# The first attention of a two-layer gated network: exponentials one step on, projections a tile ahead, a second normalisation on Pool

## The chip, the core and the metric
The kernel runs on one core of a Trainium2 chip. The metric is the device time of one execution in microseconds (us), lower is better. The engines of the core work side by side, each through its own list of instructions in order, and wait for one another through counters (semaphores): TensorE (PE) does matrix products and transposes, VectorE (DVE) and ScalarE (ACT) do work per element, GpSimd (Pool) does slower work per element, and SyncE (SP) issues transfers.

## What is computed
The whole program is a network of two layers, each with a cross-attention and a feed-forward part, on 32 x 64 tokens of width 256. The change touches the first cross-attention alone:

```python
x = x + tanh(g_xattn[0]) * xattn0(layernorm(x), ctx, ctx, W_q, W_k, W_v, W_o)

def xattn0(XQ, XK, XV, Wq, Wk, Wv, Wo):      # projections mix the 64 rows of a batch entry
    q, k, v = heads(Wq @ XQ), heads(Wk @ XK), heads(Wv @ XV)     # 8 heads of 32 columns
    p = softmax(q @ k.T / sqrt(32))
    return Wo @ (XQ - p @ v)
```

So the normalised rows of x are needed twice: once early, for the queries, and once late, where the attention is subtracted from them.

## The kernel before
The 2048 tokens are 16 tiles of 128 rows (two batch entries each). `attention0` (from L303) runs the tiles as a software pipeline. Each engine has a function `step(s)`, which issues what belongs to tile s, and, for the tiles before, t = s-1 and u = s-2; on VectorE n = s+1 is the next tile. `run_steps` (L75) calls it for the first steps, then in a hardware loop over pairs of steps, then for the last ones. Nothing but these functions sets the order: an engine does its instructions as they are written, and waits at each `after(...)` until the counter named there has come far enough.

One tile passes through these operations, whose names are used below:
- **xn** (DVE, L590 through L175): normalised rows for the queries. **Q/K** (PE, L530): projections of queries and keys, 8 matmul instructions. **V** (PE, L536): projection of the values.
- **q_t, k_m** (ACT, L474 and L478): queries and keys from PSUM to SBUF. **v_m** (one half on DVE, L603, one on ACT, L491): the values.
- **scores** (PE, L551), **smax** and **shifted** (DVE, L609 and L612), **prob** (ACT, L500): exponentials. **den, rden** (DVE, L596 and L598): sums and their reciprocals.
- **transposes of prob** (PE, L543), **p_t** (ACT, L483), **out** (PE, L563), **head** (DVE, L638).
- **xn_late** (ACT, L485): the second normalisation, **mix** (Pool, L454): the difference, **proj** (PE, L571), **x_all** and **stats** (DVE, L643 and L645): the residual and the statistics of the next norm.

Beside this, ACT and Pool split the context into two parts for the second attention (k_hi, L496; k_lo, L440), Pool splits the weights of the feed-forward part (w_hi and w_lo, L445 and L447), and SP loads the context and stores the parts. At step 2 the norm of the tiles from 4 on is computed (L617 on DVE, with a square root on ACT at L505).

In a step before the change PE does Q/K(s), V(s), transposes(t), scores(s), out(t), proj(u). ACT does q_t and k_m(s), p_t(t), xn_late(t), v_m(s), k_hi(s), prob(s). DVE does den and rden(t), v_m(s), xn(n), smax and shifted(s), head(t), x_all and stats(u).

Of the kernel before, what the change touches and what calls it, by code (L numbers as in the profile page):

```python
# [10 lines left out]
ALU = mybir.AluOpType  # L11
# [63 lines left out]
def run_steps(eng, body, count, lag, unroll, head=0):  # L75

    head = max(head, -(-lag // unroll))
    tail = count // unroll  # L80
    for n in range(head * unroll):
        body(Step(n // unroll, n % unroll, unroll))
    with eng.Fori(head, tail) as r:
        for slot in range(unroll):
            body(Step(r, slot, unroll))
    for n in range(tail * unroll, count + lag):
        body(Step(n // unroll, n % unroll, unroll))
# [215 lines left out]
def attention0(nc, sem, keep, d):  # L303
# [5 lines left out]
    with ExitStack() as ctx:  # L309
# [103 lines left out]
        def _(pool):  # L413
# [20 lines left out]
            def step(s):  # L434
                if s.inside(TILES):
# [12 lines left out]
                t = s.plus(-1)  # L448
                if t.inside(TILES):

                    after(pool, late_ready, t)
# [8 lines left out]
        def _(act):  # L460
# [8 lines left out]
            def step(s):  # L469
# [10 lines left out]
                if t.inside(TILES):  # L480
                    after(act, pt_done, t)
                    after(act, o_done, t.plus(-2))
                    act.activation(p_t[:, t.slot], pt_ps[:], ACT.Copy).then_inc(pt_ready, 1)  # L483
                    after(act, mix_ready, t.plus(-2))
                    act.activation(xn_late[:, t.slot], at(x_all, t.n), ACT.Identity, bias=column(norm.shift, t.n),  # L485
                                   scale=column(norm.rstd, t.n)).then_inc(late_ready, 1)
                if s.inside(TILES):
                    after(act, v_done, s)
# [4 lines left out]
                if s.inside(TILES):  # L493
                    after_dma(act, ctx_loaded, s)
                    after_dma(act, kop_written, s.plus(-2), 3)
                    act.activation(k_hi[:, s.slot], ctx_t[:, s.slot], ACT.Copy).then_inc(khi_ready, 1)  # L496
                    after(act, shift_ready, s)
                    after(act, pt_done, s.plus(-2))
                    after(act, den_ready, s.plus(-2))
                    act.activation(prob[:, s.slot], shifted[:, s.slot], ACT.Exp, scale=SCALE0).then_inc(prob_ready, 1)  # L500
                    if s.known and s.n == 0:
                        act.wait_ge(gate_loaded, 48)
                        act.activation(gates[:], gate_in[:, 0:4], ACT.Tanh).then_inc(gate_steps, 1)
                    if s.known and s.n == 2:
                        norm.scalar(act, slice(GT, XT))  # L505
# [5 lines left out]
        def _(pe):  # L511
# [6 lines left out]

            def step(s):
                t, u = s.plus(-1), s.plus(-2)  # L520
                if s.inside(TILES):

                    after(pe, xn_ready, s)
                    after_dma(pe, ctx_loaded, s)
                    after(pe, q_ready, s.plus(-2))
                    after(pe, k_ready, s.plus(-2))
                    for m, src in ((0, xn), (1, ctx_t)):
                        for c in range(DC):
                            o = (2 * m + c) * P
                            mm = pe.matmul(qk_ps[s.slot][:, o:o + P], lhsT=src[:, s.slot, c * P:(c + 1) * P], rhs=w_t[:, m],  # L530
                                           start=True, stop=True)
                    mm.then_inc(qk_done, 1)
                    after(pe, v_ready, s.plus(-1))
                    after(pe, v_odd_ready, s.plus(-1))
                    for b in range(2):
# [1628 lines left out]
```

## Time and profile before
| | |
|---|---|
| median of 3 runs | 675.91 us (674.12 to 676.22) |
| profiled execution | 673.21 us, of which 671.5 us are the span |
| first attention | from the start to about 106 us |
| loop over tile pairs, steps 4 to 15 | about 40 to 101 us |
| busy of each step of 5.12 us (two steps, 41.0 to 51.3 us, halved) | PE 4.40, DVE 4.15, ACT 4.35, Pool 2.89 us |

The trace gives for each group of instructions its start, its length, its engine and its line; in square brackets stands how long the engine was idle before it and what ended that. "issue" is idle time for which the profile shows no releaser. A group of several instructions starts with the first and ends with the last. The matmul clock that the chip granted was full speed from 40 to 90 us, and 0.89 and 0.77 of it in the two stretches of 5 us before that.

### The profile page before, as it was taken

How to read it: one execution, taken by the hardware profiler on the slowest of the kernel's cores; microseconds unless marked ns; L12 is line 12 of the kernel's file. 1: busy time of each engine (PE TensorE's matmuls, PEld its weight loads, DVE VectorE, ACT ScalarE, POOL GpSimd, SP SyncE). 2: the span in 40 equal slices, each digit the busy share in tenths (PEclk: the TensorE clock that was granted, in tenths of full speed). 3: DMA queues.
4: the chain of work that ended last, by engine and by line, in shares of the span. 5: the costliest groups of instructions: out<-in, count | busy, mean ns of one | idle time of the engine just before them, and what ended most of it. 6: DMA issues, size and time to landing. Idle time of an engine off the chain costs nothing. (4 is left out here: it accounts for less than half of the span.)

```text
span 671.5 us, 16680 instructions
## 1 busy us (share of the span) xinstructions
PE 603.9 (90%) x4997; PEld 460.1 (69%) x4997; DVE 489.4 (73%) x999; ACT 404.1 (60%) x829; POOL 313.0 (47%) x430
## 2 busy tenths in 40 slices
PE   3688877999999966999999999999789699999995
PEld 2577765788888865655555555555478599999884
DVE  2877886788978796598899999996556634444756
ACT  3888884344434441488898888998645145555431
POOL 2455555023222557934675765753237334024254
PEclk9989997999999987699999999999969889999998
DMA  5434438400000014344444444440002435446344
GB/s 163 114 99 130 130 105 290 155 1 1 0 0 1 23 50 137 106 132 130 129 145 127 138 139 123 143 139 29 2 1 75 130 102 187 145 150 189 109 141 127
DMA packets 72601, 71.20 MB, mean 106 GB/s; under 512 B 12364, under 2 KB 68812, under 8 KB 72556
## 3 DMA queue, kind: packets, MB, share of 16 engines
q1 hardware_dynamic: 67324, 56.33, 28.2%
q0 software_dynamic: 5232, 14.29, 6.9%
q8 instruction: 25, 0.41, 0.3%
q14 instruction: 20, 0.16, 0.1%
HBM read 38.48 MB, written 31.36 MB: 104 GB/s over the span
## 5 line engine op out<-in xcount | busy, mean ns | idle before, releaser
L1420 DVE TENSOR_REDUCE a_smax<-a_s 128x2 f32<-128x512 f32 x256 | 164.7, 681 | 19.9 <-PE a_s L1348 15.1
L1242 ACT ACTIVATE a_prob<-a_st 128x512 f32<-128x512 f32 x256 | 141.8, 597 | 23.8 <-PE a_st L1343 22.7
L1348 PE MATMUL a_s<-kop,qop 64*128 64x256 f32 x512 | 106.3, 324 | 5.6 <-DVE a_smax L1420 3.4
L1343 PEld LDWEIGHTS a_st<-qop,kop 64*128 64x128 f32 x512 | 70.8, 187 | 56.8 <-issue 24.9
L1343 PE MATMUL a_st<-qop,kop 64*128 64x256 f32 x512 | 104.0, 315 | 0.6 <-DVE a_smax L1420 0.5
L1303 PE MATMUL a_pv<-a_prob,a_vt 128*32 128x256 f32 x1024 | 81.6, 391 | 3.2 <-ACT a_pv_sb L1227 1.7
L819 POOL TENSOR_TENSOR f_hs_lo<-f_kept,f_hs_hi 128x512 fp32r<-128x512 f32 x32 | 41.3, 1320 | 85.5 <-ACT f_hs_hi L769 85.5
L1348 PEld LDWEIGHTS a_s<-kop,qop 64*128 64x128 f32 x512 | 73.0, 193 | 7.9 <-DVE a_smax L1420 4.8
L1871 POOL DMA_INDIRECT sorted_rows<-m_xn,m_slot x32 | 33.5, 1047 | 46.1 <-PE m_gu L128 26.6
L126 PE MATMUL f_bank<-f_xt_hi,w_hi 128*128 128x512 f32 x128 | 51.2, 400 | 1.1 <-DVE w_raw L865 0.6
L127 PE MATMUL f_bank<-f_xt_lo,w_hi 128*128 128x512 f32 x128 | 50.5, 395 | 0.0
L128 PE MATMUL f_bank<-f_xt_hi,w_lo 128*128 128x512 f32 x128 | 50.3, 393 | 0.0
L787 ACT ACTIVATE f_mag<-w_raw 128x512 f32<-128x512 f32 x32 | 20.2, 633 | 44.5 <-DVE w_raw L865 44.5
L1181 POOL TENSOR_TENSOR we_lo<-we_raw,we_hi 128x176 f32 (+3 forms) x24 | 16.5, 688 | 61.5 <-DMA qop<-qop_rows 57.6
L126 PE MATMUL f_bank<-wd_hi,f_hs_hi 128*128 128x256 f32 x128 | 37.4, 292 | 6.3 <-POOL f_hs_lo L819 6.2
L1887 POOL DMA_INDIRECT m_xn<-expert_rows,m_slot x16 | 15.9, 993 | 54.5 <-DMA expert_rows<-turned 39.5
L865 DVE TENSOR_TENSOR w_raw<-f_sg,f_bank 128x512 f32<-128x512 f32 x32 | 21.9, 684 | 21.3 <-ACT f_sg L783 15.6
L127 PE MATMUL f_bank<-wd_lo,f_hs_hi 128*128 128x256 f32 x128 | 36.9, 288 | 0.0
L128 PE MATMUL f_bank<-wd_hi,f_hs_lo 128*128 128x256 f32 x128 | 36.9, 288 | 0.0
L1303 PEld LDWEIGHTS a_pv<-a_prob,a_vt 128*32 128x32 f32 x1024 | 20.6, 107 | 22.1 <-ACT a_pv_sb L1227 3.7
L783 ACT ACTIVATE f_sg<-f_bank 128x512 f32<-128x512 f32 x32 | 18.7, 585 | 27.0 <-PE f_bank L128 27.0
L440 POOL TENSOR_TENSOR k_lo<-ctx_t,k_hi 128x256 fp32r<-128x256 f32 x16 | 11.7, 729 | 47.2 <-ACT k_hi L496 34.9
(263 smaller groups left out, 1663.4 us busy)
## 6 DMA issues: line engine op xcount, KB each, us to landing
qop<-qop_rows SPq DMA_DIRECT2D x64, 100.0 KB
kop<-kop_rows SPq DMA_DIRECT2D x64, 96.0 KB
sorted_rows<-x_all SPq DMA_DIRECT2D x2, 2944.0 KB, 15.4
qop<-sorted_rows SPq DMA_DIRECT2D x46, 128.0 KB, 2.3
expert_rows<-turned SPq DMA_DIRECT2D x46, 128.0 KB
kop_rows<-k_hi SPq DMA_DIRECT2D x32, 128.0 KB, 2.3
qop_rows<-q_hi POOLq DMA_DIRECT2D x30, 128.0 KB, 2.7
x_all<-in_x SPq DMA_DIRECT2D x4, 512.0 KB, 5.8
```

The costliest lines, as they stand in the source:

```text
L126: pe.matmul(out, lhsT=lh, rhs=rh, start=first, stop=False, **kw)
L127: pe.matmul(out, lhsT=lh, rhs=rl, start=False, stop=False, **kw)
L128: return pe.matmul(out, lhsT=ll, rhs=rh, start=False, stop=last, **kw)
L787: act.activation(mag[:, j], hid[:, c, j], ACT.Abs).then_inc(mag_ready, 1)
L819: pool.tensor_tensor(hs[1][:, j], kept[:, j], raw(hs[0][:, j]), ALU.subtract).then_inc(hs_ready, 1)
L865: dve.tensor_tensor(hid[:, c, j], sg[:, j % 2], u_ps[j % 2][:], ALU.mult).then_inc(hid_ready, 1)
L1242: act.activation(prob[:, u % 8], st_ps[BANK[u]][:], ACT.Exp, scale=SCALE1).then_inc(prob_ready, 1)
L1303: mm = pe.matmul(pv_ps[v4 * 32:(v4 + 1) * 32, 0:D], lhsT=vt[:, w_.slot, c, u], rhs=prob[:, u % 8, c * D:(c + 1) * D], start=(c == 0), stop ...
L1343: st = pe.matmul(st_ps[BANK[u]][:, c * D:(c + 1) * D], lhsT=kop[t.slot][rows, u // 2, c * P:(c + 1) * P], rhs=qop[t.slot][rows, u // 2], s ...
L1348: sm = pe.matmul(s_ps[BANK[u]][:, c * D:(c + 1) * D], lhsT=qop[v.slot][rows, w // 2, c * P:(c + 1) * P], rhs=kop[v.slot][rows, w // 2], st ...
L1420: dve.tensor_reduce(smax[:, v.slot, opposite(u)], s_ps[BANK[u]][:].rearrange("p (q n) -> p q n", q=2), AX_X, ALU.max).then_inc(smax_ready, 1)
L1871: pool.indirect_dma_start(out=d["sorted"][b], out_offset=bass.IndirectOffsetOnAxis(ap=slot[:, k, t:t + 1], axis=0), in_=xn[:, t], in_offse ...
```

## The change
It has four parts.
- PE issues Q/K and V of tile n = s+1 within step s: Q/K(n) behind scores(s), V(n) behind transposes(t). Those of tile 0 stand ahead of the steps, and `run_steps` ends the loop one pair earlier on PE (`ahead=2`).
- ACT issues prob for t = s-1 instead of s, right behind q_t and k_m(s). k_hi and v_m follow, and p_t(t) is last.
- xn_late leaves ACT. Pool makes it from two operations (a product with 1/std and a sum with the shift), at the start of its step.
- DVE issues den and rden(t) behind shifted(s) instead of at the start of the step.

```diff
--- before.py
+++ after.py
@@ -72,12 +72,12 @@
         return not self.known or 0 <= self.n < count
 
 
-def run_steps(eng, body, count, lag, unroll, head=0):
+def run_steps(eng, body, count, lag, unroll, head=0, ahead=0):
 
 
 
     head = max(head, -(-lag // unroll))
-    tail = count // unroll
+    tail = (count - ahead) // unroll
     for n in range(head * unroll):
         body(Step(n // unroll, n % unroll, unroll))
     with eng.Fori(head, tail) as r:
@@ -432,6 +432,14 @@
             pool.memset(norm.eps[:], EPS).then_inc(ident_steps, 1)
 
             def step(s):
+                t = s.plus(-1)
+                if t.inside(TILES):
+                    after(pool, xn_ready, t)
+                    after(pool, mix_ready, t.plus(-2))
+                    scale, shift = (column(c, t.n).to_broadcast([P, D]) for c in (norm.rstd, norm.shift))
+                    pool.tensor_tensor(xn_late[:, t.slot], at(x_all, t.n), scale, ALU.mult).then_inc(late_ready, 1)
+                    after(pool, late_ready, t, 2, 1)
+                    pool.tensor_tensor(xn_late[:, t.slot], xn_late[:, t.slot], shift, ALU.add).then_inc(late_ready, 1)
                 if s.inside(TILES):
                     after_dma(pool, w0_loaded, s)
 
@@ -445,10 +453,9 @@
                     pool.tensor_copy(w0[0][:, m, :, :, n], src).then_inc(w0_hi, 1)
                     after(pool, w0_hi, s)
                     pool.tensor_tensor(w0[1][:, m, :, :, n], src, raw(w0[0][:, m, :, :, n]), ALU.subtract).then_inc(w0_lo, 1)
-                t = s.plus(-1)
                 if t.inside(TILES):
 
-                    after(pool, late_ready, t)
+                    after(pool, late_ready, t, 2)
                     after(pool, head_ready, t)
                     after(pool, proj_done, t.plus(-2))
                     pool.tensor_tensor(mix[:, t.slot], xn_late[:, t.slot], head[:, t.slot], ALU.subtract).then_inc(mix_ready, 1)
@@ -478,31 +485,28 @@
                         op = act.activation(k_m[r, s.slot, :, :, h], src, ACT.Copy)
                     op.then_inc(k_ready, 1)
                 if t.inside(TILES):
-                    after(act, pt_done, t)
-                    after(act, o_done, t.plus(-2))
-                    act.activation(p_t[:, t.slot], pt_ps[:], ACT.Copy).then_inc(pt_ready, 1)
-                    after(act, mix_ready, t.plus(-2))
-                    act.activation(xn_late[:, t.slot], at(x_all, t.n), ACT.Identity, bias=column(norm.shift, t.n),
-                                   scale=column(norm.rstd, t.n)).then_inc(late_ready, 1)
+                    after(act, shift_ready, t)
+                    after(act, pt_done, t.plus(-2))
+                    after(act, den_ready, t.plus(-2))
+                    act.activation(prob[:, t.slot], shifted[:, t.slot], ACT.Exp, scale=SCALE0).then_inc(prob_ready, 1)
+                    if t.known and t.n == 0:
+                        act.wait_ge(gate_loaded, 48)
+                        act.activation(gates[:], gate_in[:, 0:4], ACT.Tanh).then_inc(gate_steps, 1)
                 if s.inside(TILES):
+                    after_dma(act, ctx_loaded, s)
+                    after_dma(act, kop_written, s.plus(-2), 3)
+                    act.activation(k_hi[:, s.slot], ctx_t[:, s.slot], ACT.Copy).then_inc(khi_ready, 1)
                     after(act, v_done, s)
                     after(act, o_done, s.plus(-2))
                     for out, src in v_copies(s, 1):
                         op = act.activation(out, src, ACT.Copy)
                     op.then_inc(v_odd_ready, 1)
-                if s.inside(TILES):
-                    after_dma(act, ctx_loaded, s)
-                    after_dma(act, kop_written, s.plus(-2), 3)
-                    act.activation(k_hi[:, s.slot], ctx_t[:, s.slot], ACT.Copy).then_inc(khi_ready, 1)
-                    after(act, shift_ready, s)
-                    after(act, pt_done, s.plus(-2))
-                    after(act, den_ready, s.plus(-2))
-                    act.activation(prob[:, s.slot], shifted[:, s.slot], ACT.Exp, scale=SCALE0).then_inc(prob_ready, 1)
-                    if s.known and s.n == 0:
-                        act.wait_ge(gate_loaded, 48)
-                        act.activation(gates[:], gate_in[:, 0:4], ACT.Tanh).then_inc(gate_steps, 1)
-                    if s.known and s.n == 2:
-                        norm.scalar(act, slice(GT, XT))
+                if t.inside(TILES):
+                    after(act, pt_done, t)
+                    after(act, o_done, t.plus(-2))
+                    act.activation(p_t[:, t.slot], pt_ps[:], ACT.Copy).then_inc(pt_ready, 1)
+                if s.known and s.n == 2:
+                    norm.scalar(act, slice(GT, XT))
 
             run_steps(act, step, TILES, 2, 2, 2)
             norm.scalar(act, EARLY)
@@ -516,32 +520,31 @@
             pe.transpose(banks[1][:, 0:P], w_raw[:, 4], ident[:]).then_inc(wt_done, 1)
             pe.wait_ge(wt_ready, 1)
 
+            def queries_and_keys(n):
+                if not n.inside(TILES):
+                    return
+                after(pe, xn_ready, n)
+                after_dma(pe, ctx_loaded, n)
+                after(pe, q_ready, n.plus(-2))
+                after(pe, k_ready, n.plus(-2))
+                for m, src in ((0, xn), (1, ctx_t)):
+                    for c in range(DC):
+                        o = (2 * m + c) * P
+                        mm = pe.matmul(qk_ps[n.slot][:, o:o + P], lhsT=src[:, n.slot, c * P:(c + 1) * P], rhs=w_t[:, m],
+                                       start=True, stop=True)
+                mm.then_inc(qk_done, 1)
+
+            def values(n):
+                if not n.inside(TILES):
+                    return
+                after(pe, v_ready, n.plus(-1))
+                after(pe, v_odd_ready, n.plus(-1))
+                for b in range(2):
+                    mm = pe.matmul(v_ps[:, b * D:(b + 1) * D], lhsT=w_t[:, 3 + b], rhs=ctx_t[:, n.slot], start=True, stop=True)
+                mm.then_inc(v_done, 1)
+
             def step(s):
-                t, u = s.plus(-1), s.plus(-2)
-                if s.inside(TILES):
-
-                    after(pe, xn_ready, s)
-                    after_dma(pe, ctx_loaded, s)
-                    after(pe, q_ready, s.plus(-2))
-                    after(pe, k_ready, s.plus(-2))
-                    for m, src in ((0, xn), (1, ctx_t)):
-                        for c in range(DC):
-                            o = (2 * m + c) * P
-                            mm = pe.matmul(qk_ps[s.slot][:, o:o + P], lhsT=src[:, s.slot, c * P:(c + 1) * P], rhs=w_t[:, m],
-                                           start=True, stop=True)
-                    mm.then_inc(qk_done, 1)
-                    after(pe, v_ready, s.plus(-1))
-                    after(pe, v_odd_ready, s.plus(-1))
-                    for b in range(2):
-                        mm = pe.matmul(v_ps[:, b * D:(b + 1) * D], lhsT=w_t[:, 3 + b], rhs=ctx_t[:, s.slot], start=True, stop=True)
-                    mm.then_inc(v_done, 1)
-                if t.inside(TILES):
-
-                    after(pe, prob_ready, t)
-                    after(pe, pt_ready, t.plus(-1))
-                    for hp in range(4):
-                        mm = pe.transpose(pt_ps[:, hp * P:(hp + 1) * P], prob[:, t.slot, hp * P:(hp + 1) * P], ident[:])
-                    mm.then_inc(pt_done, 1)
+                t, u, n = s.plus(-1), s.plus(-2), s.plus(1)
                 if s.inside(TILES):
                     after(pe, q_ready, s)
                     after(pe, k_ready, s)
@@ -553,6 +556,15 @@
                                            rhs=k_m[:, s.slot, c, b].rearrange("p h e -> p (h e)"),
                                            start=True, stop=True, tile_position=(0, b * SEQ))
                     mm.then_inc(score_done, 1)
+                queries_and_keys(n)
+                if t.inside(TILES):
+
+                    after(pe, prob_ready, t)
+                    after(pe, pt_ready, t.plus(-1))
+                    for hp in range(4):
+                        mm = pe.transpose(pt_ps[:, hp * P:(hp + 1) * P], prob[:, t.slot, hp * P:(hp + 1) * P], ident[:])
+                    mm.then_inc(pt_done, 1)
+                values(n)
                 if t.inside(TILES):
                     after(pe, pt_ready, t)
                     after(pe, v_ready, t)
@@ -570,7 +582,9 @@
                     after(pe, x_ready, u.plus(-1))
                     pe.matmul(proj_ps[:, 0:D], lhsT=w_t[:, 2], rhs=mix[:, u.slot], start=True, stop=True).then_inc(proj_done, 1)
 
-            run_steps(pe, step, TILES, 2, 2)
+            queries_and_keys(Step(0, 0, 2))
+            values(Step(0, 0, 2))
+            run_steps(pe, step, TILES, 2, 2, ahead=2)
 
         @block.vector
         def _(dve):
@@ -591,11 +605,6 @@
 
             def step(s):
                 t, u, n = s.plus(-1), s.plus(-2), s.plus(1)
-                if t.inside(TILES):
-                    after(dve, prob_ready, t)
-                    dve.tensor_reduce(den[:, t.slot], prob[:, t.slot].rearrange("p (h e) -> p h e", h=H0), AX_X, ALU.add).then_inc(den_ready, 1)
-                    after(dve, den_ready, t)
-                    dve.reciprocal(rden[:, t.slot], den[:, t.slot]).then_inc(rden_ready, 1)
                 if s.inside(TILES):
                     after(dve, v_done, s)
                     after(dve, o_done, s.plus(-2))
@@ -612,6 +621,11 @@
                     dve.tensor_tensor(shifted[:, s.slot].rearrange("p (h e) -> p h e", h=H0),
                                       s_ps[s.slot][:].rearrange("p (h e) -> p h e", h=H0),
                                       smax[:, s.slot].unsqueeze(2).to_broadcast([P, H0, SEQ]), ALU.subtract).then_inc(shift_ready, 1)
+                if t.inside(TILES):
+                    after(dve, prob_ready, t)
+                    dve.tensor_reduce(den[:, t.slot], prob[:, t.slot].rearrange("p (h e) -> p h e", h=H0), AX_X, ALU.add).then_inc(den_ready, 1)
+                    after(dve, den_ready, t)
+                    dve.reciprocal(rden[:, t.slot], den[:, t.slot]).then_inc(rden_ready, 1)
                 if s.known and s.n == 2:
                     dve.wait_ge(stats0, TILES)
                     norm.vector(dve, slice(GT, XT), lambda: finished(t, u))
```

What stands on PE in one step of the loop, before. The rows are instructions in order: the line, the operation, the tile written and the ones read, and the shape.
```order
L530 MATMUL a_bank<-w_t,xn 128x128 x2
L530 MATMUL a_bank<-w_t,ctx_t 128x128 x2
L536 MATMUL a_bank<-ctx_t,w_t 128x256 x2
L543 MATMUL a_bank<-ident,prob 128x128 x4
L551 MATMUL a_bank<-k_m,q_t 64x256 x4
L563 MATMUL a_bank<-v_m,p_t 64x64 x8
L571 MATMUL a_bank<-mix,w_t 128x256
```
And after the change (L554 scores, L533 Q/K, L565 transposes, L543 V, L575 out, L583 proj; the ISA rows are the registers and waits of the loop):
```order
L554 MATMUL a_bank<-k_m,q_t 64x256 x4
L94 ISA
L101 ISA
L533 MATMUL a_bank<-w_t,xn 128x128 x2
L533 MATMUL a_bank<-w_t,ctx_t 128x128 x2
L565 MATMUL a_bank<-ident,prob 128x128 x4
L543 MATMUL a_bank<-ctx_t,w_t 128x256 x2
L575 MATMUL a_bank<-v_m,p_t 64x64 x8
L583 MATMUL a_bank<-mix,w_t 128x256
```
Scores come first in the step; Q/K stands behind scores and V behind the transposes, both for the next tile.

What stands on DVE from x_all of one step on into the next, before:
```order
L643 SCALAR_TENSOR_TENSOR x_all<-a_bank,gates,x_all 128x256
L645 ISA
L645 BN_STATS stats<-x_all 128x6
L596 TENSOR_REDUCE den<-prob 128x8
L598 RECIPROCAL rden<-den 128x8
L94 REGISTER_ALU
L603 COPY v_m<-a_bank 64x4x32 x2
L175 ISA x2
L175 TENSOR_SCALAR xn<-x_all,ln_rstd,ln_shift 128x256
L609 TENSOR_REDUCE smax<-a_bank 128x8
```
And after the change (L657 x_all, L659 stats, L612 v_m, L175 xn, L618 smax, L621 shifted, L626 and L628 the sums and reciprocals):
```order
L657 SCALAR_TENSOR_TENSOR x_all<-a_bank,gates,x_all 128x256
L659 ISA
L659 BN_STATS stats<-x_all 128x6
L94 REGISTER_ALU
L612 COPY v_m<-a_bank 64x4x32 x2
L175 ISA x2
L175 TENSOR_SCALAR xn<-x_all,ln_rstd,ln_shift 128x256
L618 TENSOR_REDUCE smax<-a_bank 128x8
L621 TENSOR_TENSOR shifted<-a_bank,smax 128x512
L626 TENSOR_REDUCE den<-prob 128x8
L628 RECIPROCAL rden<-den 128x8
```
The sums and reciprocals have moved from between stats and v_m to behind shifted. xn stands where it stood, behind v_m and ahead of smax, and it is still for tile s+1, which PE now takes in step s.

## Rows read from the trace of the kernel before
**Rows 1.** timeline at 66 us, first path: start us, length us, engine, line
```profile
65.64 1.08 PE L551 MATMUL a_bank<-k_m,q_t 128*64 128x256 f32 x8 [0.76 <-issue]
...
66.76 0.69 DVE L609 TENSOR_REDUCE smax<-a_bank 128x8 f32<-128x512 f32 x1 [0.83 <-PE a_bank L551]
...
67.48 0.69 DVE L612 TENSOR_TENSOR shifted<-a_bank,smax 128x512 f32<-128x512 f32 x1
...
68.21 0.63 ACT L500 ACTIVATE prob<-shifted 128x512 f32<-128x512 f32 x1 [0.66 <-DVE shifted L612]
...
68.86 0.38 ACT L474 ACTIVATE q_t<-a_bank 128x256 f32<-128x256 f32 x1
...
69.14 1.52 ACT L478 ACTIVATE k_m<-a_bank 32x256 f32<-32x256 f32 x4
...
70.69 0.60 ACT L483 ACTIVATE p_t<-a_bank 128x512 f32<-128x512 f32 x1
```

**Rows 2.** timeline, the scores of step 4 (loop entry)
```profile
40.02 1.08 PE L551 MATMUL a_bank<-k_m,q_t 128*64 128x256 f32 x8 [0.73 <-issue]
```

**Rows 3.** timeline, same step, rest of the matmul engine
```profile
66.52 0.66 PE L563 MATMUL a_bank<-v_m,p_t 128*64 128x64 f32 x16
...
67.12 0.70 PE L571 MATMUL a_bank<-mix,w_t 128*128 128x256 f32 x2
...
67.65 0.61 PE L530 MATMUL a_bank<-w_t,xn 128*128 128x128 f32 x4
...
68.10 0.61 PE L530 MATMUL a_bank<-w_t,ctx_t 128*128 128x128 f32 x4
...
68.54 1.03 PE L536 MATMUL a_bank<-ctx_t,w_t 128*128 128x256 f32 x4
...
69.41 0.60 PE L543 MATMUL a_bank<-ident,prob 128*128 128x128 f32 x4
```

**Rows 4.** timeline, same step, rest of the vector engine
```profile
68.09 0.41 DVE L638 TENSOR_TENSOR head<-a_bank,rden 128x256 f32<-128x256 f32 x1
...
68.42 0.47 DVE L643 SCALAR_TENSOR_TENSOR x_all<-a_bank,gates,x_all 128x256 f32 x1
...
69.04 0.43 DVE L645 BATCH_NORM_STATS2 stats<-x_all  x1
...
69.45 0.69 DVE L596 TENSOR_REDUCE den<-prob 128x8 f32<-128x512 f32 x1
...
70.37 0.48 DVE L603 COPY v_m<-a_bank 64x128 f32<-64x128 f32 x2
...
70.78 0.40 DVE L175 TENSOR_SCALAR xn<-x_all,ln_rstd,ln_shift 128x256 f32 x1
```

**Rows 5.** timeline, same step, Pool
```profile
67.63 0.73 POOL L440 TENSOR_TENSOR k_lo<-ctx_t,k_hi 128x256 fp32r<-128x256 f32 x1 [1.99 <-ACT k_hi L496]
...
69.14 0.86 POOL L447 TENSOR_TENSOR w_lo<-w_raw,w_hi  x1 [0.17 <-POOL w_hi L445]
...
69.96 0.73 POOL L454 TENSOR_TENSOR mix<-xn_late,head 128x256 f32<-128x256 f32 x1
```

**Rows 6.** timeline, the same form of Pool operation at 264 us
```profile
264.49 0.61 POOL L203 TENSOR_TENSOR q_lo<-x_all,ln_rstd 128x256 f32<-128x256 f32 x1
```

**Rows 7.** timeline, 478 us, two normalisations with Pool idle
```profile
478.32 0.74 DVE L175 TENSOR_SCALAR a_vt<-x_all,ln_rstd,ln_shift 128x256 f32<-128x256 f32 x2
```

**Rows 8.** timeline, 479 us, the next two, with Pool at work
```profile
478.97 1.73 DVE L175 TENSOR_SCALAR a_vt<-x_all,ln_rstd,ln_shift 128x256 f32<-128x256 f32 x2
479.01 0.73 POOL L1199 TENSOR_TENSOR a_att<-a_back 128x256 f32<-128x256 f32 x1 [5.56 <-ACT a_back L1254]
...
479.82 0.72 POOL L1201 TENSOR_TENSOR x_all<-x_all,a_att 128x256 f32<-128x256 f32 x1
```

**Rows 9.** timeline, step 3 before the loop
```profile
31.09 0.31 ACT L171 ACTIVATE ln_std<-ln_var,eps 128x13 f32<-128x13 f32 x1
...
33.32 1.44 PE L551 MATMUL a_bank<-k_m,q_t 128*64 128x256 f32 x8 [2.43 <-issue]
```

## Prediction
> **What bounds the kernel now.** I read the windows first. From 40 to 90 us no engine is full: in a step of 5.12 us all four compute engines have idle time, so a chain through several engines sets the pace. Then the timeline of one step, in which the brackets name the waits. [rows 1] are that chain: prob (start 68.21) to q_t 0.65, q_t to k_m 0.28, k_m 1.52, k_m's end (70.66) to the next scores 0.10, scores to smax 1.12, smax to shifted 0.72, shifted to prob 0.73. The sum is 5.12 us. From the scores of step 4 at 40.02 [rows 2] to those at 65.64 [rows 1] are five steps of 5.12 us, so the chain closes. It is closed because ACT does prob(s) ahead of q_t and k_m(s+1). The reader should see in [rows 1] that ACT waits 0.66 us for shifted and PE 0.76 us ahead of the scores.
>
> **What the change removes.** prob moves to the next step, behind k_m, so shifted has a whole step to be ready and that chain is open. xn_late leaves ACT, which is not the limit then. These edits give nothing by themselves: what counts is which chain is longest next.
>
> **What is late next: ACT and PE.** p_t(t) is last in ACT's step and waits for transposes(t), which now stand behind scores(s) and Q/K(n); the next q_t stands behind p_t. Lengths from [rows 1, 3]: scores 0.88 (65.64 to 66.52), Q/K 0.89 (67.65 to 68.54), transposes 0.60 and 0.04 to ACT (as from the end of the scores to smax), p_t 0.62 with its hand-over, q_t 0.28, k_m 1.52, to the scores 0.10. Sum 4.93 us, 0.19 less than today. V, k_hi and v_m lie beside it.
>
> **What is late next: xn.** DVE issues xn(n) where it did, behind v_m(s), and that is behind x_all and stats of the step before. Today PE takes xn a step later. Now Q/K(n) wants it in step s, 0.88 us after scores(s) start. x_all(u) waits for proj(u), the last thing in PE's step. So a chain closes: Q/K(n), transposes, V, out, proj, x_all, stats, v_m, xn, next Q/K. Its terms, by [rows 3, 4]:
> Q/K 0.89; transposes 0.45 (not seen with a successor; four matmuls of that shape take 0.45 from 67.65 to 68.10, and at most the 0.60 they last); V 0.87 (68.54 to 69.41); out 0.60 (66.52 to 67.12); proj 0.70 and 0.04 to DVE; x_all to stats 0.62 (68.42 to 69.04); stats to its successor 0.41 (69.04 to 69.45); v_m to xn 0.41 (70.37 to 70.78); xn 0.40; to PE 0.07 (between the 0.04 and the 0.10 above).
> Sum 5.46 us, 0.34 more than today. Queued behind the waiting Q/K on PE are transposes, V, out and proj, and behind these p_t, head and x_all; so the wait costs its full length. den and rden, 0.92 us from 69.45 to 70.37 in [rows 4], have left this stretch; without that move it would be 6.4. They now stand in the time in which DVE waits for out.
>
> **Pool.** Its four operations take 3.06 us, from 67.63 to 70.69 in [rows 5]. xn_late adds two. The same form lasts 0.61 [rows 6], mix of this size 0.73 [rows 5], and the second waits 0.17 for the first, as w_lo does for w_hi [rows 5]. That makes 4.5 to 4.7 us, under 5.46, and mix is wanted only one step later. So Pool's time is hidden, but not its place beside xn. [rows 7] show two operations of xn's kind with Pool idle: 0.74 us. [rows 8] show the next two with Pool at work: 1.73 us. 
> Where does xn fall? Count from the start of head, 0.70 after out starts (0.66 and 0.04). x_all follows at 0.64 (0.60 + 0.70 + 0.04 - 0.70), xn at 0.64 + 0.62 + 0.41 + 0.41 = 2.08. Pool: head 0.41, 0.04 to 0.17 to Pool (the two signal times above), mix 0.73, first half of xn_late 0.61 to 0.73, 0.17: the second half starts at 1.96 to 2.21. xn is held if that is under 2.12, which is about the middle. When held, xn ends 0.15 behind that half, at 2.72 to 3.00 instead of 2.48: 0.24 to 0.52 us more, around 0.35. The two halves of the unrolled loop have different register work, so one parity may be held and the other not. I take half of the steps at 0.3, on average 0.15: a step of 5.61 us. Bounds: 5.46 free, 5.98 held each time at the longest.
>
> **Sum.** From scores(4) to scores(15) are 11 steps: 11 x (5.61 - 5.12) = 5.4 us. Before them: the square root of the norm at step 2 stands ahead of q_t(3) on ACT, and scores(3) follow it [rows 9]. Its vector part now stands behind den and rden, 0.92 us. I take 0.9; bounds 0 (if the slow stretch of the clock around 33 us, scores of 1.44 us in [rows 9], hides it) and 1.8 (if the later out(0) costs as much again). After them: x_all and stats(13), 0.62 and 0.41, now stand ahead of den(15); I take 0.5, bounds 0 and 1.0. What follows the first attention starts when all engines have left it, so a shift there is passed on whole. Total +6.8 us: 673.2 of the profiled execution becomes 680.0. That execution was 2.7 us under the median of the runs, to which the sum is added: 675.9 + 6.8 = **682.7 us**, 1.0% slower. The forecast's own range, with xn held in few or in most steps, is 680 to 685.
>
> **Rivals.**
> - Pool holds xn in every step. For it: [rows 8], and the interval above lies more below 2.12 than above if mix's 0.73 is the right length. Against: the 0.61 of [rows 6], and that a held xn starts the next head late and Pool with it, so nothing draws the two together or apart. 11 x (5.81 - 5.12) + 1.4 = +9.0: 684.9 us.
> - Not slower: xn is not on the path and the ACT-PE chain of 4.93 us rules. Then 11 x -0.19 + 1.4 = -0.7: 675.2 us, no change. This needs proj's end to xn's end, 1.95 us with its signals, to shrink under about 1.4; that is the point where it decides. For it: PE has never waited for xn in a step of the trace. Against: all terms are read from rows, and DVE's list has no freedom.
> - Both chains are cut shorter by slack that I don't see, and Pool at 4.6 us becomes the bound: 11 x -0.5 + 1.4 = -4.3, 671.6 us. For it: every engine's own work is under 4.7 us. Against: the same as above.
> - The matmul clock falls to the lower of its levels, since PE idles some 1.4 us in a step (5.61 less 4.22 of its own starts) rather than 0.76. As in [rows 9], scores go from 1.08 to 1.44; the PE terms of the chain (2.81 us) grow by a third, 0.9 us a step: about 693 us. Against: the clock stayed at full speed in the loop with the 0.76 us gap, and I expect none over 1 us.
>
> **Chances.** Forecast 0.60, Pool in every step 0.22, no change 0.10, Pool-bound 0.06, clock 0.02. A measurement of this kernel can tell about 0.3%, 2 us, from no change. So slower 0.84, within 0.3% 0.10, faster 0.06. The range of 8 in 10 is 677 to 687: it leaves out the two faster rivals and the clock, and covers the bounds of the held case.
>
> **What would show it.** PE's first Q/K matmul in each loop step is released by xn (DVE), after a wait of 0.4 us or more; scores follow k_m with a gap; steps are 5.4 to 5.8 us apart, perhaps alternating; prob has no wait for shifted; xn lasts 0.40 in some steps and 0.6 to 0.9 in others. It is wrong if Q/K follows scores without a gap, if steps are under 5.3 us, or if PE waits for mix or p_t instead.

## The result and the profile after

The changed kernel takes 689.46 us, the median of 4 runs (687.48 to 690.87), against 675.47 us of the kernel before beside it. The ratio is 1.0207 (95% interval 1.0176 to 1.0238): 14 us slower. I had said 682.7, with 677 to 687 as the range. The sign and the mechanism were right, but the size, +6.8 us, was half of what came.

Where it went, by the starts of the scores (PE) and of the first matmul of the feed-forward part:

| | before | after | difference |
|---|---|---|---|
| scores of step 4 | 40.02 | 39.79 | -0.2 |
| scores of step 15 | 96.39 | 107.83 | |
| 11 steps | 56.37 (5.12 each) | 68.04 (6.19 each) | +11.7 |
| scores 15 to the feed-forward part | 10.04 | 11.78 | +1.7 |
| span | 671.5 | 685.7 | +14.2 |

13.2 us lie in the first attention; 1.0 us is left for all the rest, less than single executions of one kernel differ (687.48 to 690.87 us).

One step of the loop, from the timeline of the changed kernel (start, length, engine, line; these answer to [rows 1, 3 to 5]):
```profile
60.43 0.68 PE L533 MATMUL a_bank<-w_t,xn 128*128 128x128 f32 x4 [1.13 <-DVE xn L175]
...
61.39 0.60 PE L565 MATMUL a_bank<-ident,prob 128*128 128x128 f32 x4
...
61.83 1.03 PE L543 MATMUL a_bank<-ctx_t,w_t 128*128 128x256 f32 x4
62.03 0.60 ACT L507 ACTIVATE p_t<-a_bank 128x512 f32<-128x512 f32 x1 [2.49 <-PE a_bank L565]
...
62.79 0.69 PE L575 MATMUL a_bank<-v_m,p_t 128*64 128x64 f32 x16
...
63.40 0.70 PE L583 MATMUL a_bank<-mix,w_t 128*128 128x256 f32 x2
63.58 0.42 DVE L652 TENSOR_TENSOR head<-a_bank,rden 128x256 f32<-128x256 f32 x1 [1.24 <-PE a_bank L575]
...
64.25 0.48 DVE L657 SCALAR_TENSOR_TENSOR x_all<-a_bank,gates,x_all 128x256 f32 x1 [0.25 <-PE a_bank L583]
64.34 0.63 ACT L491 ACTIVATE prob<-shifted 128x512 f32<-128x512 f32 x1
...
64.57 1.08 PE L554 MATMUL a_bank<-k_m,q_t 128*64 128x256 f32 x8 [0.47 <-ACT k_m L485]
...
64.87 0.43 DVE L659 BATCH_NORM_STATS2 stats<-x_all  x1
...
65.38 0.48 DVE L612 COPY v_m<-a_bank 64x128 f32<-64x128 f32 x2
65.61 0.61 POOL L442 TENSOR_TENSOR xn_late<-xn_late,ln_shift 128x256 f32<-128x256 f32 x1 [0.17 <-POOL xn_late L440]
65.78 0.58 DVE L175 TENSOR_SCALAR xn<-x_all,ln_rstd,ln_shift 128x256 f32 x1
...
66.70 0.68 PE L533 MATMUL a_bank<-w_t,xn 128*128 128x128 f32 x4 [1.05 <-DVE xn L175]
...
71.88 0.63 POOL L442 TENSOR_TENSOR xn_late<-xn_late,ln_shift 128x256 f32<-128x256 f32 x1 [0.16 <-POOL xn_late L440]
71.88 0.77 DVE L175 TENSOR_SCALAR xn<-x_all,ln_rstd,ln_shift 128x256 f32 x1
...
72.89 0.68 PE L533 MATMUL a_bank<-w_t,xn 128*128 128x128 f32 x4 [1.13 <-DVE xn L175]
```
The chain can be read downward: Q/K, transposes, V, out, proj, x_all, stats, v_m, xn, and Q/K again at 66.70, released by xn after 1.05 us of idle time. prob (64.34) no longer waits for shifted. In both parities (the two steps that one pass of the loop contains) xn overlaps Pool's L442, the second half of xn_late: 0.58 and 0.77 us instead of 0.40.

The waits between 45 and 95 us (engine and line, whom it waited for, total, times, longest):
```profile
POOL mix L461 <- PE a_bank L583: 13.7, 8, 1.8
...
DVE head L652 <- PE a_bank L575: 11.6, 9, 1.3
PE a_bank L533 <- DVE xn L175: 8.7, 8, 1.2
```
Eight times Q/K waited for xn, 1.09 us in the mean. In the step of before the scores were the only place at which PE waited ([rows 1], 0.76 us); head and mix now wait in their turn, head for out and mix for head. (The row of mix names proj, L583, but the proj that mix needs is two steps old; mix starts at 64.14, 0.14 us behind the end of head.)

### The profile page after: what moved, and what is told of

It is laid out like the page before. It is cut to its first block and busy times, and to the rows that moved or that the text cites. A ratio compares the mean times of both kernels' runs of the same rounds, so it can differ in the third digit from the quotient of the medians.

```text
span 685.7 us, 16745 instructions
## 1 busy us (share of the span) xinstructions
PE 609.2 (89%) x4997; PEld 455.5 (66%) x4997; DVE 492.9 (72%) x999; ACT 393.4 (57%) x813; POOL 333.5 (49%) x462
## 5 line engine op out<-in xcount | busy, mean ns | idle before, releaser
L126 PE MATMUL m_gu<-we_hi,turned_hi 128*128 x92 | 32.4, 352 | 0.7 <-issue 0.7
```

The source lines that it names most:

```text
L126: pe.matmul(out, lhsT=lh, rhs=rh, start=first, stop=False, **kw)
```

## The experiments

Each kernel differs from the changed one unless it says otherwise. "Step" is the distance of scores 4 and 15 divided by 11. Times are medians; the ratio is to the kernel before on the same chip. The steps come from one profiled execution each. Where the intervals of two ratios overlap (the changed kernel with experiments 2 and 3; experiments 8, 9 and 10), the whole times do not tell the kernels apart, and only the steps and the rows of the traces do.

| | step | median us | ratio, 95% interval |
|---|---|---|---|
| 1. xn for tile s+2, earlier | 5.08 | 674.01 | 0.9998 (0.9979 to 1.0016) |
| 2. xn_late back on ACT | 6.04 | 686.94 | 1.0195 (1.0166 to 1.0223) |
| 3. late waits last | 6.00 | 686.48 | 1.0171 (1.0144 to 1.0198) |
| 4. Pool yields to xn | 5.90 | 684.82 | 1.0134 (1.0095 to 1.0174) |
| 5. Pool yields, late waits last | 5.72 | 683.17 | 1.0110 (1.0080 to 1.0141) |
| 6. before, with xn_late on Pool | 5.12 | 675.36 | 0.9991 (0.9972 to 1.0011) |
| 7. without the projections ahead | 6.39 | 699.47 | 1.0387 (1.0343 to 1.0431) |
| 8. xn earlier, transposes first, xn_late on ACT | 4.66 | 669.11 | 0.9928 (0.9903 to 0.9952) |
| 9. as 8, xn_late on Pool | 4.66 | 670.19 | 0.9917 (0.9888 to 0.9946) |
| 10. as 8, late waits last | 4.62 | 670.38 | 0.9942 (0.9920 to 0.9963) |

**1. xn taken off the chain.** DVE makes xn for tile s+2 ahead of head, where it waits for out anyway.
```diff
-                t, u, n = s.plus(-1), s.plus(-2), s.plus(1)
+                t, u, n = s.plus(-1), s.plus(-2), s.plus(2)
...
-                    normalise(n)
                     after(dve, score_done, s)
...
+                    if n.inside(TILES):
+                        normalise(n)
                     finished(t, u)
...
             normalise(Step(0, 0, 2))
+            normalise(Step(0, 1, 2))
...
-            run_steps(dve, step, TILES, 2, 2, 2)
+            run_steps(dve, step, TILES, 2, 2, 2, ahead=2)
```

> The changed kernel, with the first normalisation xn issued on DVE for tile s+2 ahead of head(t), in the gap of 1.2 us in which DVE waits for out, instead of for tile s+1 behind v_m. Theory (the chain proj, x_all, stats, v_m, xn, Q/K sets the step of 6.19 us): that chain is open, the chain of scores, Q/K, transposes, p_t, q_t, k_m rules with 4.93 us and some 0.1 to 0.2 of slower hand-overs, so a step of 5.0 to 5.2 us and 676 to 678 us in all, 12 us less than the changed kernel. Rival (Pool's longer work or its shared port sets the step, xn only follows): xn's place changes little, steps stay above 5.9 us and the time at 687 us or more.

Measured: 674.01 us and a step of 5.08. The timeline of this kernel around one Q/K:
```profile
71.94 0.65 DVE L175 TENSOR_SCALAR xn<-x_all,ln_rstd,ln_shift 128x256 f32 x1
...
73.46 1.08 PE L554 MATMUL a_bank<-k_m,q_t 128*64 128x256 f32 x8 [0.31 <-issue]
...
74.47 0.71 PE L533 MATMUL a_bank<-w_t,xn 128*128 128x128 f32 x4
```
xn ends at 72.59, 1.9 us ahead of the Q/K behind it, and that Q/K has no wait. xn is still held (0.65 us here), and it costs nothing. So the chain through xn set the step. The whole edit is the place of one instruction; it gives back all 14 us, and shows as well that the change without this fault would have been no change in time: the chain of scores, Q/K, transposes, p_t, q_t and k_m takes over at 5.08, as the prediction's second chain with its 4.93 said.

**2. xn_late back on ACT.** Pool loses the two operations, ACT gets the old one behind v_m:
```diff
                     op.then_inc(v_odd_ready, 1)
+                if t.inside(TILES):
+                    after(act, mix_ready, t.plus(-2))
+                    act.activation(xn_late[:, t.slot], at(x_all, t.n), ACT.Identity, bias=column(norm.shift, t.n),
+                                   scale=column(norm.rstd, t.n)).then_inc(late_ready, 1)
```

> The changed kernel, with xn_late back on ACT, behind k_hi and v_m in a stretch in which ACT waits 2.5 us for the transposes; Pool has its four operations of before. Theory (Pool's second half of xn_late holds xn by 0.18 and 0.37 us in the two parities, on the chain that sets the step): xn lasts 0.40 us each time, the step falls by 0.28 us on average to 5.9, the whole by 3 us to about 686. Rival (the hold is hidden, since Q/K waits for something else that comes as late): step 6.19 and 689 us as before.

Measured: step 6.04, 686.94 us: half of what I expected. Its timeline shows why:
```profile
66.46 0.72 POOL L441 TENSOR_TENSOR k_lo<-ctx_t,k_hi 128x256 fp32r<-128x256 f32 x1 [0.48 <-ACT k_hi L491]
...
66.81 0.52 DVE L175 TENSOR_SCALAR xn<-x_all,ln_rstd,ln_shift 128x256 f32 x1
```
k_lo has moved up into the gap, and xn, started at 66.81, ends 0.15 us behind k_lo instead of behind xn_late. So the hold is not tied to xn_late.

**3. Late waits last.** Nothing but the order of wait instructions:
```diff
-                after(pe, xn_ready, n)
                 after_dma(pe, ctx_loaded, n)
                 after(pe, q_ready, n.plus(-2))
                 after(pe, k_ready, n.plus(-2))
+                after(pe, xn_ready, n)
```
The same was done ahead of out (p_t's last) and head (out's last).

> The changed kernel; only the order of the wait instructions is different: ahead of Q/K the wait for xn stands last instead of first of four, ahead of out the wait for p_t last instead of first of four, ahead of head the wait for out last. Theory (the hand-over from xn to Q/K of 0.24 to 0.34 us and that from p_t to out of 0.16 us are long because three more waits are worked off after the late one): they fall to about 0.1 us, the step by 0.2 to 0.3 us, the whole by 2 to 3 us to about 686.5. Rival (the hand-over is what a signal takes, weights first): nothing moves, 689 us.

Measured: step 6.00, 686.48 us. Timeline of this kernel:
```profile
64.97 0.63 DVE L175 TENSOR_SCALAR xn<-x_all,ln_rstd,ln_shift 128x256 f32 x1
...
65.65 0.71 PE L533 MATMUL a_bank<-w_t,xn 128*128 128x128 f32 x4 [0.81 <-DVE xn L175]
...
67.28 0.60 ACT L507 ACTIVATE p_t<-a_bank 128x512 f32<-128x512 f32 x1 [2.36 <-PE a_bank L565]
...
68.04 0.68 PE L575 MATMUL a_bank<-v_m,p_t 128*64 128x64 f32 x16
```
xn ends at 65.60 and Q/K starts 0.05 us later, where the changed kernel took 0.24 to 0.34 (xn's end at 66.36, Q/K at 66.70). So in the loop the place of the late wait among these four is worth 0.2 to 0.3 us at this link, and 0.19 us of the step. For out it made no difference: p_t's end at 67.88 to 68.04 is 0.16 in both. That half of the theory failed, and what these 0.16 us are stays open.

The last Q/K stands outside the hardware loop, and there the same edit went the other way. First the changed kernel, with xn's wait first:
```profile
103.17 0.60 DVE L175 TENSOR_SCALAR xn<-x_all,ln_rstd,ln_shift 128x256 f32 x1
...
103.82 0.71 PE L533 MATMUL a_bank<-w_t,xn 128*128 128x128 f32 x4 [0.94 <-DVE xn L175]
```
Then experiment 3, with xn's wait last:
```profile
101.35 0.63 DVE L175 TENSOR_SCALAR xn<-x_all,ln_rstd,ln_shift 128x256 f32 x1
...
102.13 0.68 PE L533 MATMUL a_bank<-w_t,xn 128*128 128x128 f32 x4 [1.07 <-DVE xn L175]
```
The link is 0.05 us in the first and 0.15 us in the second. So waits that are met already have no price of their own that holds everywhere. In the loop the waits compare with values from registers, outside it with constants; whether that makes the difference was not tried.

**4. Pool yields.** One wait more on Pool:
```diff
                     after(pool, late_ready, t, 2, 1)
+                    if s.inside(TILES):
+                        after(pool, xn_ready, s.plus(1))
                     pool.tensor_tensor(xn_late[:, t.slot], xn_late[:, t.slot], shift, ALU.add).then_inc(late_ready, 1)
```

> The changed kernel with one wait more: Pool starts the second half of xn_late only when DVE has finished xn, so that no Pool operation runs at that moment; Pool has the time (it waits 1.7 us for head in each step). Putting xn_late back on ACT only moved k_lo into the place of that half, and xn was still held to 0.52 and 0.61 us. Theory (what holds xn is whichever Pool operation runs beside it): xn lasts 0.40 us each time, the step falls from 6.19 to 5.9, the whole by 3 us to 686 to 687. Rival (xn is long for another reason, as the dynamic address or reading beside the matmul engine): xn stays at 0.58 and 0.77, the step at 6.19 or longer by the wait.

Measured: step 5.90, 684.82 us. Groups of its instructions between 41 and 95 us:
```profile
L175 DVE TENSOR_SCALAR xn<-x_all,ln_rstd,ln_shift 128x256 f32 x9 | 3.6, 396 | 0.0
...
L444 POOL TENSOR_TENSOR xn_late<-xn_late,ln_shift 128x256 f32<-128x256 f32 x9 | 5.5, 612 | 7.1 <-DVE xn L175 7.1
```
xn is at 0.396 us in the mean (0.645 in the changed kernel), and the step fell by that quarter of a microsecond and a little more. A wait added to Pool made the kernel faster than the changed one.

**5. Both.** Edits 3 and 4 together.

> The changed kernel with both: Pool yields to xn, and the late waits stand last ahead of Q/K, out and head (which alone gave a step of 6.00). Theory (hold and hand-over are separate terms of one chain): a step of 5.70 to 5.75 us, 5 us less than the changed kernel, 684 us; this is my predicted chain of 5.46 plus what remains of slower hand-overs. Rival (shortening one lets another chain show): above 5.85.

Measured: step 5.72, 683.17 us. The two terms add up: 0.29 and 0.19 alone, 0.47 together.

**6. The Pool part alone, in the kernel before.** There PE takes xn a step later.

> The kernel before with one part of the change alone: xn_late made by two operations on Pool, not on ACT. Theory (xn is off the path there, since PE takes it a step later, and ACT gets to v_m and k_hi earlier but still waits for shifted): step 5.12 and 674 to 675 us, no change, although xn may be held by Pool. Rival (the shared port costs DVE on any path): slower by 2 us or more.

Measured: 675.36 us, ratio 0.9991, step 5.12. The two operations on Pool are free in themselves. xn happened not to be held here (0.397 us in the mean), so this run doesn't show a held xn off the path; experiment 1 does. Here Pool was the one held: its second half took 0.666 us in the mean instead of 0.61.

**7. Without the projections ahead.** PE's step as before the change, the other three parts kept.

> The changed kernel with PE's order of before: Q/K and V of the tile of the step, not of the next. So exponentials one step on, den one place later and xn_late on Pool remain. Theory (these parts need the projections ahead: otherwise Q/K, q_t, k_m, prob, transposes, p_t, out and proj stand in one row): Q/K to q_t 1.05, q_t and k_m 1.80, prob 0.65, then v_m and k_hi until p_t starts and out behind it 1.76, proj 0.6, to Q/K 0.55, a step of 6.4 us, 11 x 1.3 us over the kernel before, 689 to 693 us. Rival (taking prob off the old chain pays by itself): steps of 5.1 us or less, 675 us.

Measured: step 6.39, and 699.47 us, beyond my range. The timeline of this kernel:
```profile
63.75 0.38 ACT L481 ACTIVATE q_t<-a_bank 128x256 f32<-128x256 f32 x1 [3.96 <-PE a_bank L534]
...
65.58 0.63 ACT L491 ACTIVATE prob<-shifted 128x512 f32<-128x512 f32 x1
...
66.26 0.66 PE L547 MATMUL a_bank<-ident,prob 128*128 128x128 f32 x4 [1.68 <-ACT prob L491]
...
68.86 0.61 PE L534 MATMUL a_bank<-w_t,xn 128*128 128x128 f32 x4
...
70.04 0.38 ACT L481 ACTIVATE q_t<-a_bank 128x256 f32<-128x256 f32 x1 [2.44 <-PE a_bank L534]
```
From one q_t (63.75) to the next (70.04) are 6.29 us: k_m, prob, transposes, p_t, out, proj, Q/K in one row. The step's mean is longer since one of the eleven, from 59.04 to 66.84, took 7.8 us. From 60 to 62 us the granted clock was 0.50, the lower of its two levels; in the 8 us before 58 PE had been busy for 5.0 us at full speed. The loop explains 14 us of the 25, and the scores of step 4 stand 6.5 us later than before, with a clock of 0.77 from 40 to 45 us. The 4.4 us between that and the median I leave open; the runs of this kernel also spread from 695 to 705.

**8. Both chains open.** Edit 1, xn_late on ACT, and on PE
```diff
                     mm.then_inc(score_done, 1)
-                queries_and_keys(n)
...
                     mm.then_inc(pt_done, 1)
+                queries_and_keys(n)
                 values(n)
```

> The changed kernel with three edits: xn for tile s+2 ahead of head, xn_late back on ACT, and on PE the transposes ahead of Q/K of the next tile. Theory (both chains are then open: scores, transposes, p_t, q_t, k_m is 4.1 us): the fullest engines rule, PE 4.3, ACT 4.5 and DVE 4.3 us with waits, so steps of 4.5 to 4.7 us and 668 to 671 us, faster than both kernels. Rival (a third chain through mix, proj and x_all or through head closes at 5 us): 675 us or more.

Measured: step 4.66, 669.11 us, faster than the kernel before by 0.7%. Busy times of its engines in a stretch of 45 us (PE, PE's weights, DVE, ACT, Pool):
```profile
45.00:90.00 45.00, 44.71 (x409) 31.77 (x410) 39.89 (x96) 41.82 (x107) 27.44 (x39) 1.00 0.50 140
```
PE is busy in 44.71 of 45 us: now an engine sets the step, and in its timeline from 65 to 76 us no matmul group has a wait ahead of it.

**9. The same with xn_late on Pool.** This keeps all four parts of the change.

> The changed kernel with two edits: xn for tile s+2 ahead of head, and transposes ahead of Q/K on PE; xn_late stays on Pool. With xn_late on ACT as well this gave steps of 4.66 us. Theory (Pool's six operations of 4.6 us and their waits are then as long as the step): steps of 4.7 to 4.9 us, 670 to 672 us. Rival (Pool's work is hidden and ACT, relieved of 0.6 us, lets the step fall): under 4.6 us, 668 us.

Measured: step 4.66, 670.19 us. Groups of its instructions, 41 to 95 us:
```profile
L175 DVE TENSOR_SCALAR xn<-x_all,ln_rstd,ln_shift 128x256 f32 x10 | 6.7, 669 | 0.5
...
L442 POOL TENSOR_TENSOR xn_late<-xn_late,ln_shift 128x256 f32<-128x256 f32 x12 | 7.3, 612 | 2.0 <-POOL xn_late L440 2.0
```
PE is the limit here too (busy for 44.65 us of 45 to 90), not Pool (39.01). The mean of xn, 0.669 us, hides two cases:
```profile
58.66 0.41 DVE L175 TENSOR_SCALAR xn<-x_all,ln_rstd,ln_shift 128x256 f32 x1
58.81 0.99 POOL L455 TENSOR_TENSOR w_lo<-w_raw,w_hi  x1 [0.18 <-POOL w_hi L453]
...
81.64 0.85 POOL L455 TENSOR_TENSOR w_lo<-w_raw,w_hi  x1 [0.18 <-POOL w_hi L453]
81.71 0.94 DVE L175 TENSOR_SCALAR xn<-x_all,ln_rstd,ln_shift 128x256 f32 x1
```
In five of the ten xn starts behind w_lo and is held (0.82 to 0.98 us); in the other five it starts 0.15 to 0.27 us ahead of w_lo and takes 0.41, and in four of these w_lo is the one held (0.96 to 0.99 us instead of 0.85). Nobody waits for xn in either case. The step came out just under what I expected of Pool's load (4.7 to 4.9), so Pool's 4.6 us of work are covered.

**10. And late waits last, on all of PE.**

> The fastest version so far (xn for tile s+2 ahead of head, transposes ahead of Q/K, xn_late on ACT; steps of 4.66 us) with the late waits last everywhere on PE and for head on DVE. Theory (PE is full there, and the order of waits that are already met costs the same in any order, only the late ones gain): k_m to scores 0.1 instead of 0.25 in one parity, a step of 4.6 us, 0.5 to 1 us less in all, 668.5 us. Rival (each PE group follows its predecessor, no wait is late): nothing, 669 us.

Measured: step 4.62 as the theory had it, but 670.38 us against 669.11 with intervals that overlap. No gain can be told.

## Why the prediction was wrong in size

The chain through xn that I put forward is the one that sets the step; experiment 1 shows it. What failed are sizes in its sum: the hand-over from xn to Q/K, put at 0.07 us and measured at 0.24 to 0.34, and Pool's hold, put at 0.15 us a step and measured at 0.18 and 0.37. Of the 7.4 us between the forecast of +6.8 and the +14.2 of the span, the loop makes 6.3 and the tail 1.2, the head takes back 1.1, and 1.0 lies behind the first attention, where I had none. The chain's terms, predicted and measured in the two parities of the timeline above (the second parity runs from Q/K at 66.70 to 72.89; its middle rows are not shown):

| term | predicted | first | second |
|---|---|---|---|
| Q/K to transposes | 0.89 | 0.96 | 0.97 |
| transposes to V | 0.45 | 0.44 | 0.43 |
| V to out | 0.87 | 0.96 | 0.96 |
| out to proj | 0.60 | 0.61 | 0.62 |
| proj to x_all | 0.74 | 0.85 | 0.84 |
| x_all to stats, v_m, xn | 1.44 | 1.53 | 1.36 |
| xn | 0.40 + 0.15 | 0.58 | 0.77 |
| xn to Q/K | 0.07 | 0.34 | 0.24 |
| sum | 5.61 | 6.27 | 6.19 |

**Hand-overs.** "To PE 0.07 (between the 0.04 and the 0.10 above)" is the term that was most off: it was 0.24 to 0.34. I bounded it by two hand-overs of the trace of before, neither of which was to a group with four waits of which the first is the late one. Experiment 3 shows that the order of the four waits makes 0.2 us or more of it in the loop. V to out is longer since p_t, and not V, is what out waits for: transposes 0.60, to ACT 0.04, p_t 0.60 and the 0.16 behind it are the 1.40 us from 61.39 to 62.79. I had left p_t beside the chain. Q/K takes 0.07 to 0.08 more behind scores and a wait. What makes proj to x_all 0.1 longer was not tried, nor why the stretch from x_all to xn is 0.09 longer in one parity and 0.08 shorter in the other. Together these are 0.63 us in the first parity and 0.36 in the second, some 5 us over the loop: more than the hold.

**Pool's hold.** "I take half of the steps at 0.3" failed: it was held in ten of the eleven steps, all but the first of the loop, by 0.18 and 0.37 us in turn, 0.28 in the mean instead of 0.15, another 1.2 us over the loop. That is the rival "Pool holds xn in every step", which got 0.22. The shorter hold lies under my bounds of a held xn (0.24 to 0.52). The argument that near ties fall to both sides failed too. Counted from the start of head, Pool's second half starts at 2.03 us in both parities (63.58 to 65.61, 69.85 to 71.88), inside my 1.96 to 2.21 but without spread; xn starts at 2.20 in the first, where I had 2.08, and at 2.03 in the second, which is a tie, and ties are lost. Experiment 4 takes it out: 0.29 us a step, 3 us in all. Experiment 5, with neither hold nor late wait, has 5.72 us, still 0.26 over the 5.46 of the free case: Q/K's longer group, p_t ahead of out, and proj to x_all.

**The 11 steps** were the right count: 68.04 - 56.37 = 11.7 us instead of 5.4.

**Head.** I took +0.9; it was -0.2. The scores of step 3 came 1.3 us later (34.61 instead of 33.32), as the working said, but the slow stretch of the clock did not come. The windows of the changed kernel (the last four numbers are Pool's count, the granted clock, the DMA share and GB/s):
```profile
30.00:35.00 5.00, 3.07 (x32) 2.20 (x32) 3.90 (x15) 4.31 (x9) 2.76 (x4) 1.00 0.50 136
35.00:40.00 5.00, 4.78 (x44) 3.28 (x41) 2.85 (x6) 4.87 (x12) 2.44 (x4) 1.00 0.18 42
```
The clock is at 1.00 in both where before had 0.89 and 0.77, and step 3 to 4 takes 5.2 us instead of 6.7. PE was idle for 1.93 us ahead of those scores, before for 2.43 [rows 9]. This is luck of one execution and no property of the change: in the traces of experiments 2 to 5 PE was as busy from 30 to 35 us (3.07 us), and yet the clock was at 0.68 to 0.79 from 35 to 40 us, step 3 to 4 took 6.75 to 6.85 us, and the scores of step 4 came at 40.11 to 41.70, later than before by 0.1 to 1.7 us. In the trace of experiment 6, whose PE order is that of before, the clock stayed at 1.00 and these scores came at 38.53. So the head can't be told from the change to better than about 1.5 us, and the +0.9 is neither confirmed nor refuted by the -0.2.

**Tail.** I took 0.5 of at most 1.0 for x_all and stats ahead of den; it was 1.7. What I had missed is that v_m, and an xn for a tile behind the last one, which nobody reads and which takes 0.77 us beside Pool, stand between the last scores and their smax:
```profile
107.83 1.08 PE L554 MATMUL a_bank<-k_m,q_t 128*64 128x256 f32 x8 [0.30 <-issue]
...
109.03 0.77 DVE L175 TENSOR_SCALAR xn<-x_all,ln_rstd,ln_shift 128x256 f32 x1
...
109.73 0.67 DVE L618 TENSOR_REDUCE smax<-a_bank 128x8 f32<-128x512 f32 x1
...
113.19 0.69 PE L575 MATMUL a_bank<-v_m,p_t 128*64 128x64 f32 x16 [0.69 <-ACT p_t L507]
...
115.20 0.42 DVE L652 TENSOR_TENSOR head<-a_bank,rden 128x256 f32<-128x256 f32 x1
```
smax starts 0.82 us behind the end of the scores; in [rows 1] it was 0.04. That is the first half of the 1.7. The other is the term that I had, at its upper bound: the last den and the vector part of the next norm stand ahead of the last head, which starts 1.32 us behind the end of out, and in the kernel before 0.28 us (101.69 to 101.97).

**Where the expected gain went.** The rival "not slower" had it at 4.93 us a step if xn were not on the path; with xn moved the step is 5.08. So opening the old chain was worth next to nothing alone, since the new one through p_t is as long. Only with the transposes ahead of Q/K, experiments 8 and 9, does the change pay.

## What to carry to other kernels

When a consumer is moved a step ahead, move its producer a step ahead too, and look for the idle gap of that engine: here one instruction's place was worth 14 us. Where a chain is summed from durations, each link between engines needs a price from a link of its own kind, and an operation that stands beside the chain (p_t here) must be checked against the term that it could replace: 0.05 us at each of eight terms is 4.4 us over eleven steps. And where two engines may collide on a critical chain, a start within a few hundredths of a microsecond is better priced as lost for VectorE, or taken out by a wait on the other engine.

## What the runs showed of the hardware

- In the loop, the place of a late wait among four changed the time from xn's end to the first Q/K matmul: 0.24 to 0.34 us with it first, 0.05 to 0.06 with it last. From p_t to out it was 0.16 us either way, and at the last Q/K, outside the loop, it was 0.05 with it first and 0.15 with it last. So there is no fixed price for a wait, and the reason stays open.
- A DVE tensor-by-scalar operation from SBUF to SBUF that ran into a Pool operation ended 0.14 to 0.16 us behind it, whichever it was: 66.36 behind 66.22 (xn_late), 72.65 behind 72.51, 67.33 behind 67.18 (k_lo), 82.65 behind 82.49 (w_lo). The Trainium skill (SBUF — State Buffer, "Who interferes with whom") has this as an exclusive lock, and the trace agrees in those four.
- Who wins is settled by a lead of some hundredths. The same section says "Whoever issues first gets the shared pair for the whole instruction". By the starts that the profile shows this is not enough: at 71.88 both start at the same hundredth and DVE loses, and in experiment 3 DVE starts 0.04 us ahead and loses (first two rows). In experiment 7 it starts 0.06 us ahead and wins, and Pool's operation takes 0.81 us instead of 0.61 (last two rows).
```profile
70.86 0.80 DVE L175 TENSOR_SCALAR xn<-x_all,ln_rstd,ln_shift 128x256 f32 x1
70.90 0.61 POOL L442 TENSOR_TENSOR xn_late<-xn_late,ln_shift 128x256 f32<-128x256 f32 x1 [0.16 <-POOL xn_late L440]
```
```profile
44.66 0.40 DVE L175 TENSOR_SCALAR xn<-x_all,ln_rstd,ln_shift 128x256 f32 x1
44.72 0.81 POOL L442 TENSOR_TENSOR xn_late<-xn_late,ln_shift 128x256 f32<-128x256 f32 x1 [0.17 <-POOL xn_late L440]
```
- Making Pool wait until DVE was through made the changed kernel 0.7% faster (684.82 against 689.46 us, from two sets of runs; as ratios 1.0134, 1.0095 to 1.0174, against 1.0207, 1.0176 to 1.0238: the intervals just miss each other).
